# The last layer's self-attention with its two heads on the two halves of the array's rows, the maxima added by a bf16 matmul, and the key sums on GpSimd

## What is computed

```python
def _L1_attn_ref(x, w_q, w_k, w_v, w_o):          # 16 heads, d_k = 64, no mask
    scale = 1.0 / sqrt(64)
    q = einsum('bsd,hdk->bhsk', x, w_q)           # k and v alike
    scores = einsum('bhqk,bhmk->bhqm', q, k) * scale
    weights = softmax(scores, axis=-1)
    z = einsum('bhqm,bhmk->bhqk', weights, v)
    z = transpose(z, (0, 2, 1, 3)).reshape(b, s, h * dk)
    return x + einsum('bse,ed->bsd', z, w_o)
```

## Time and profile before

| | us |
|---|---|
| timed runs, median of 3 (lowest, highest) | 914.5 (913.91, 914.62) |
| the profiled execution | 905.64 |
| its span in the trace | 903.8 |
| of it, the loop of stage d and its output (from L1218's first to L1316's start) | 366.5 to 650.8 |
| busy in the span: PE, DVE, ACT, POOL | 804.2, 563.1, 302.9, 126.6 |
| mean granted clock of TensorE in the profiled execution | 0.932 of full speed |

### The profile page before, as it was taken

The page is one execution under the profiler, slowest core; times in us unless marked ns, Lnnn a source line. Parts: engine busy times, 40 slices in busy tenths (PEclk is TensorE's granted clock), DMA queues, the critical chain, the costliest instruction groups (busy, mean ns, idle before and its releaser), DMA issues.

```text
span 903.8 us, 8453 instructions
## 1 busy us (share of the span) xinstructions
PE 804.2 (89%) x3018; PEld 390.6 (43%) x3018; DVE 563.1 (62%) x1288; ACT 302.9 (34%) x499; POOL 126.6 (14%) x116
## 2 busy tenths in 40 slices
PE   7528788879999999999999999999898698999996
PEld 4214563466665433322322322232464235466665
DVE  5979799544155494457878778778654654433334
ACT  3360656600321105434544554553103221312220
POOL 0796221300010011000000000000035310000000
PEclk9858599999997899869999999999999798999999
DMA  8000000000500000000000000000031000000000
GB/s 344 25 1 0 1 1 2 1 1 0 213 1 1 0 1 0 1 0 0 1 0 1 1 0 1 0 1 0 1 126 73 1 1 1 0 1 1 0 1 24
DMA packets 3491, 18.64 MB, mean 21 GB/s; under 512 B 887, under 2 KB 2040, under 8 KB 2938
## 3 DMA queue, kind: packets, MB, share of 16 engines
q1 hardware_dynamic: 3450, 18.11, 5.0%
HBM read 17.58 MB, written 0.52 MB: 20 GB/s over the span
## 4 chain that ended last, share of the span: by engine, by line
PE 63%; DVE 22%; POOL 6%; ACT 5%; issue 3%; DMA 0%; POOLq 0%; DVEq 0%; SPq 0%; ACTq 0%
PE PS L1759 9%; PE PS L1218 8%; DVE SB L1429 6%; PE PS L1231 5%; PE PS L1773 5%; PE PS L1185 4%; PE PS L1198 3%; PE PS L215 2%; DVE SB L1388 2%; DVE SB L1134 2%; PE PS L639 2%; PE PS L1316 2%; PE PS L1247 2%; PE PS L662 2%; PE PS L1557 1%
## 5 line engine op out<-in xcount | busy, mean ns | idle before, releaser
L1218 PE MATMUL PS<-SB 68*128 68x512 f32 x256 | 128.6, 627 | 0.0
L195 POOL TENSOR_TENSOR SB<-SB 128x4 f32<-128x4 f32 (+1 forms) x26 | 25.9, 996 | 676.9 <-DVE SB L179 676.7
L215 PE MATMUL PS<-SB 128*128 128x512 f32 (+1 forms) x232 | 108.8, 617 | 5.0 <-ACT SB L511 3.5
L1378 DVE TENSOR_REDUCE SB<-PS 128x2 f32<-128x1024 f32 x64 | 78.3, 1224 | 54.0 <-PE PS L1198 54.0
L1343 ACT ACTIVATE SB<-PS 128x1024 f32<-128x1024 f32 x64 | 65.5, 1023 | 92.1 <-PE PS L1218 90.7
L1759 PE MATMUL PS<-SB 128*128 128x512 f32 x176 | 82.5, 607 | 0.0
L1231 PE MATMUL PS<-SB 128*64 128x512 f32 x256 | 70.4, 629 | 7.7 <-DVE SB L1433 7.7
L1218 PEld LDWEIGHTS PS<-SB 68*128 68x128 f32 x256 | 46.3, 195 | 60.5 <-issue 59.2
L215 PEld LDWEIGHTS PS<-SB 128*128 128x128 f32 x232 | 45.3, 214 | 50.3 <-issue 43.0
L1839 DVE TENSOR_TENSOR SB<-SB,PS 128x512 f32<-128x512 f32 (+1 forms) x48 | 32.8, 688 | 52.7 <-PE PS L1759 49.1
L1429 DVE RECIPROCAL SB<-PS 128x512 f32<-128x512 f32 x16 | 53.7, 3358 | 7.5 <-PE PS L1247 7.0
(11 more groups left out here) (350 smaller groups left out, 1124.9 us busy)
## 6 DMA issues: line engine op xcount, KB each, us to landing
SB<-exp SPq DMA_DIRECT2D x1, 4352.0 KB, 13.3
SB<-moe SPq DMA_DIRECT2D x1, 4096.0 KB, 13.0
SB<-dft SPq DMA_DIRECT2D x1, 2304.0 KB, 11.4
SB<-att SPq DMA_DIRECT2D x1, 2048.0 KB, 16.7
SB<-mix SPq DMA_DIRECT2D x1, 768.5 KB, 4.2
SB<-mix SPq DMA_DIRECT2D x1, 640.0 KB, 5.3
SB<-ssm SPq DMA_DIRECT2D x1, 602.0 KB, 6.4
SB<-lat SPq DMA_DIRECT2D x1, 585.0 KB
```

The costliest lines, as they stand in the source:

```text
L215: pe.matmul(bank(b)[:, 0:moving.shape[1]], ones, moving, start=True, stop=True)
L1218: ins = pe.matmul(bank(2 * (n % 2) + k), two_heads(k_ring[i % 3])[0:DK + 4, h, 128 * kt:128 * kt + 128], two_heads(q_ring[i % 3])[0:DK + 4 ...
L1378: dve.tensor_reduce(shift[i % 2][:, qt:qt + 5:4], two_heads(bank(4, 2)), AX_X, ALU.max, negate=True)\
```

## The change

The two heads of a pair now stay on the partitions on which the projection leaves them, 0 to 63 and 64 to 127. ACT copies bank 7 twice, to bf16 and to f32, with no move between partitions. A score step u takes key tile u of both heads: two f32 matmuls on the two halves of the array's rows, and then two bf16 matmuls (64 rows of ones times shift_rows) into the same banks, which add the maxima. The maxima's transpose is one of 128 x 128 (shift has the columns of the first head from 0, of the second from 64, the rest zero), and DVE multiplies it with own_tile into shift_rows, all 128 partitions at once. expd is ordered by key tile, so the key sum of a pair is three additions of 1024 columns, which are now on GpSimd. PE's order changes: maxima 0, 2, 3 come right behind the scores, ahead of project and weigh, and weigh 0 comes behind maxima 1. DVE keeps its order without the key sums.

```diff
@@ -1149,10 +1149,11 @@
     D2 = Space(W2.end, END)
     headed = D2(8192)
     expd = [D2(4096) for _ in range(2)]
-    q_ring, k_ring = [D2(1024) for _ in range(3)], [D2(1024) for _ in range(3)]
-    qb_ring, kb_ring = [D2(512, BF16) for _ in range(3)], [D2(512, BF16) for _ in range(3)]
-    half_sum, key_sum, unit = D2(1024), D2(1024), D2(512)
-    shift = [D2(8) for _ in range(2)]
+    q_ring, k_ring = [D2(512) for _ in range(3)], [D2(512) for _ in range(3)]
+    qb_ring, kb_ring = [D2(256, BF16) for _ in range(3)], [D2(256, BF16) for _ in range(3)]
+    half_sums, key_sum, unit = [D2(1024) for _ in range(2)], D2(1024), D2(512)
+    shift, shift_rows = [D2(128) for _ in range(2)], [D2(256, BF16) for _ in range(2)]
+    own_tile, ones_16 = D2(4), D2(64, BF16)
     NP_ = B * PAIRS
 
     ctx_n, ctx_T, ctx_kv = lat["ctx"], xn[:, 0:512], att["w_v"]
@@ -1189,34 +1190,33 @@
             n = 4 * i + qt
             if qt == 0:
 
-                pe.wait_ge(sem("d_bf16"), 2 * i + 2)
+                pe.wait_ge(sem("d_qk_in"), 4 * i + 4)
                 if i >= 1:
                     pe.wait_ge(sem("d_shift_in"), i)
             if n >= 1:
                 pe.wait_ge(sem("d_max"), n)
             for h in range(2):
-                ins = pe.matmul(bank(4 + h), two_heads(qb_ring[i % 3])[0:DK, h, 128 * qt:128 * qt + 128],
-                                two_heads(kb_ring[i % 3])[0:DK, h, :], start=True, stop=True)
+                ins = pe.matmul(bank(4 + h), qb_ring[i % 3][head(h), 128 * qt:128 * qt + 128], kb_ring[i % 3][head(h), :],
+                                start=True, stop=True)
             ins.then_inc(sem("d_rough"), 1)
 
         def shifts(i):
 
             pe.wait_ge(sem("d_max"), 4 * i + 4)
-            for h in range(2):
-                ins = pe.transpose(bank(4)[0:4, 128 * h:128 * h + 128], shift[i % 2][:, 4 * h:4 * h + 4], ident)
-            ins.then_inc(sem("d_shifts"), 1)
+            pe.transpose(bank(4)[:, 0:128], shift[i % 2], ident).then_inc(sem("d_shifts"), 1)
 
         def score(i, u):
-            h, half = divmod(u, 2)
             n = 4 * i + u
             if u == 0:
                 pe.wait_ge(sem("d_shift_in"), i + 1)
             if n >= 2:
                 pe.wait_ge(sem("d_exp"), n - 1)
-            for k in range(2):
-                kt = 2 * half + k
-                ins = pe.matmul(bank(2 * (n % 2) + k), two_heads(k_ring[i % 3])[0:DK + 4, h, 128 * kt:128 * kt + 128],
-                                two_heads(q_ring[i % 3])[0:DK + 4, h, :], start=True, stop=True)
+            for h in range(2):
+                pe.matmul(bank(2 * (n % 2) + h), k_ring[i % 3][head(h), 128 * u:128 * u + 128], q_ring[i % 3][head(h), :],
+                          start=True, stop=False)
+            for h in range(2):
+                ins = pe.matmul(bank(2 * (n % 2) + h), ones_16[head(h), :], shift_rows[i % 2][head(h), :],
+                                start=False, stop=True)
             ins.then_inc(sem("d_scores"), 1)
 
         def weigh(i, kt):
@@ -1228,7 +1228,7 @@
                     pe.wait_ge(sem("d_headed"), i)
             for h in range(2):
                 v = value[:, 1024 * (4 * b + kt) + 128 * pair + DK * h:1024 * (4 * b + kt) + 128 * pair + DK * h + DK]
-                ins = pe.matmul(bank(6)[DK * h:DK * h + DK, :], v, expd[i % 2][:, 2048 * h + 512 * kt:2048 * h + 512 * kt + 512],
+                ins = pe.matmul(bank(6)[head(h), :], v, expd[i % 2][:, 1024 * kt + 512 * h:1024 * kt + 512 * h + 512],
                                 start=(kt == 0), stop=(kt == 3))
             if kt == 3:
                 ins.then_inc(sem("d_weighed"), 1)
@@ -1273,11 +1273,11 @@
                 project(1, 1)
             if 2 <= t < 6:
                 maxima(0, t - 2)
+        pe.wait_ge(sem("d_ones"), 3)
         shifts(0)
         stay_warm(pe, 3, 5)
         pe.wait_ge(sem("d_v_even"), NT // 2)
         pe.wait_ge(sem("d_v_odd"), NT // 2)
-        pe.wait_ge(sem("d_ones"), 3)
         for i in range(NP_ + 1):
             now, ahead, before = i < NP_, i + 1 < NP_, i >= 1
 
@@ -1286,14 +1286,12 @@
                     shifts(i + 1)
                 if now:
                     score(i, u)
-                if ahead and u in (0, 2):
-                    maxima(i + 1, (0, None, 3)[u])
-                if before:
-                    weigh(i - 1, u)
-                if ahead and u == 1:
-                    maxima(i + 1, 2)
+                if ahead and u < 3:
+                    maxima(i + 1, (0, 2, 3)[u])
                 if i + 2 < NP_ and u < 2:
                     project(i + 2, u)
+                if before and u:
+                    weigh(i - 1, u)
                 if i == NP_ - 2 and u == 1:
                     pe.wait_ge(sem("e_ctx_n"), 1)
                     pe.wait_ge(sem("d_unit"), NP_ - 3)
@@ -1304,6 +1302,8 @@
                     context(u)
                 if ahead and u == 0:
                     maxima(i + 1, 1)
+                if before and u == 0:
+                    weigh(i - 1, 0)
                 if before and u == 2:
                     sums(i - 1)
         for t in range(NT):
@@ -1329,11 +1329,8 @@
 
                 act.wait_ge(sem("d_scores"), 4 * (i - 2))
             act.wait_ge(sem("d_qk"), 2 * i + which + 1)
-            for h in range(2):
-                act.activation(two_heads(ring[i % 3])[0:DK, h, :], bank(7)[DK * h:DK * h + DK, :], ACT.Copy, scale=s)\
-                   .then_inc(sem("d_qk_in"), 1)
-            act.wait_ge(sem("d_qk_in"), 4 * i + 2 * which + 2)
-            act.activation(low[i % 3][0:DK, :], ring[i % 3][0:DK, :], ACT.Copy).then_inc(sem("d_bf16"), 1)
+            act.activation(low[i % 3], bank(7), ACT.Copy, scale=s).then_inc(sem("d_qk_in"), 1)
+            act.activation(ring[i % 3], bank(7), ACT.Copy, scale=s).then_inc(sem("d_qk_in"), 1)
 
         def exp(i, u):
             if i >= 2 and u == 0:
@@ -1362,8 +1359,20 @@
     def d_pool(pool):
 
         pool.wait_ge(sem("stage_done"), 3)
-        for r in k_ring:
-            pool.memset(r[DK:DK + 4, :], 1.0).then_inc(sem("d_ones"), 1)
+        pool.memset(ones_16, 1.0).then_inc(sem("d_ones"), 1)
+        for s in shift:
+            pool.memset(s, 0.0).then_inc(sem("d_ones"), 1)
+
+        for i in range(NP_):
+            for half in range(2):
+                pool.wait_ge(sem("d_exp"), 4 * i + 2 * half + 2)
+                e = expd[i % 2][:, 2048 * half:2048 * half + 2048]
+                pool.tensor_tensor(half_sums[half], e[:, 0:1024], e[:, 1024:], ALU.add).then_inc(sem("d_half_sum"), 1)
+            pool.wait_ge(sem("d_half_sum"), 2 * i + 2)
+            if i >= 1:
+                pool.wait_ge(sem("d_sums"), i)
+            pool.tensor_tensor(key_sum, half_sums[0], half_sums[1], ALU.add).then_inc(sem("d_key_sum"), 1)
+            pool.wait_ge(sem("d_key_sum"), i + 1)
 
     def d_dve(dve, follow):
         def v_in(t):
@@ -1375,31 +1384,20 @@
             dve.wait_ge(sem("d_rough"), n + 1)
             if qt == 0 and i >= 2:
                 dve.wait_ge(sem("d_shifts"), i - 1)
-            dve.tensor_reduce(shift[i % 2][:, qt:qt + 5:4], two_heads(bank(4, 2)), AX_X, ALU.max, negate=True)\
+            dve.tensor_reduce(shift[i % 2][:, qt:qt + DK + 1:DK], two_heads(bank(4, 2)), AX_X, ALU.max, negate=True)\
                .then_inc(sem("d_max"), 1)
 
         def shift_in(i):
 
             dve.wait_ge(sem("d_shifts"), i + 1)
-            if i >= 3:
-                dve.wait_ge(sem("d_scores"), 4 * (i - 2))
-            per_tile = lambda a: a.rearrange("p (h c) -> p h c", h=2)[:, :, None, :].to_broadcast([4, 2, 4, 128])
-            own = ident[0:4, None, 0:4, None].to_broadcast([4, 2, 4, 128])
-            dve.tensor_tensor(q_ring[i % 3][DK:DK + 4, :].rearrange("p (h t c) -> p h t c", h=2, t=4),
-                              per_tile(bank(4)[0:4, 0:256]), own, ALU.mult).then_inc(sem("d_shift_in"), 1)
-
-        def key_sums(i, h):
-            dve.wait_ge(sem("d_exp"), 4 * i + 2 * h + 2)
-            if h == 0 and i >= 1:
-                dve.wait_ge(sem("d_sums"), i)
-            e = expd[i % 2][:, 2048 * h:2048 * h + 2048]
-            follow(dve.tensor_tensor(half_sum, e[:, 0:1024], e[:, 1024:], ALU.add))
-            ins = dve.tensor_tensor(two_heads(key_sum)[:, h, :], half_sum[:, 0:512], half_sum[:, 512:], ALU.add)
-            if h:
-                ins.then_inc(sem("d_key_sum"), 1)
-            else:
-                follow(ins)
-
+            if i >= 2:
+                dve.wait_ge(sem("d_scores"), 4 * (i - 1))
+            dve.tensor_tensor(shift_rows[i % 2].rearrange("p (t c) -> p t c", t=4),
+                              bank(4)[:, None, 0:128].to_broadcast([P, 4, 128]),
+                              own_tile[:, :, None].to_broadcast([P, 4, 128]), ALU.mult).then_inc(sem("d_shift_in"), 1)
+
+        follow(dve.tensor_tensor(own_tile, ident[:, 0:4], ident[:, DK:DK + 4], ALU.add))
+        dve.wait_ge(sem("d_ones"), 3)
         v_in(1)
         maximum(0, 0)
```

(7 more changed lines are left out.)

## The result

The changed kernel takes 860.84 us in the median of four runs (853.79 to 866.99), the kernel before 914.45: a ratio of 0.939 (95% interval 0.930 to 0.948). The ratio leaves out the run of 866.99, which counts as a slow one because it lies over 1.5% above the fastest. In six more runs on another occasion the median was 866.31 against 913.65, ratio 0.946 (0.943 to 0.950). The executions of the changed kernel fall in two groups, near 855 and near 866, and the first figure is a middle between them. Of the two groups there is one profile each, and what parts these two lies ahead of the stage that the change touches: stage d begins (its first L207) at 351.30 us in the execution of 866.73 and at 338.49 in the one of 853.79.

A forecast was written before the change was run, and what follows sets the result against it. The prediction took the circle through the reciprocal, 14.9 us a pass, as the bound; gains of 1.0, 2.3, 3.9, 27.6 and 4.2 summed to 39.0 us, taken from the median 914.5 for 876, range 865 to 890.

The forecast's parts named there:

- the term of the clock: TensorE's clock in the stage: one fall, as now, at another place, priced at 8.1 us, so the sum stands.
- the carrying over to the median: From the profiled 905.64 us to the timed median 914.5, 8.9 above: the same 39 us taken off, giving 875.5.
- The bound and the circle: Loop pass: circle from maxima 1 through shifts, reciprocal, product and maximum, 14.9 us; PE waits before project (0.4) and maxima 1 (0.9).
- Scores and maxima side by side: PE slots on two row halves: a score slot with its bf16 pair 1.27 us, a maxima slot 0.31 against 0.53.
- rival F: GpSimd's key-sum adds in the loop take over 4.9 us, against 2.35 expected, and set the pass; chance 0.01.
- Ahead of the loop and the first passes: Before the twelve passes: gains of about 1.0 us ahead of the loop, 2.3 in the first pass, 3.9 in the second.
- D: Loop: kernel slower, the clock falling again and again, each fall taking back 8.1 us; chance 0.05.
- E: Loop: row halves don't run side by side when groups around them differ; 17.9 us a pass, 924 in all; chance 0.01.
- G: Loop: the circle through the reciprocal is shorter and PE's 13.6 us sets the pass, giving 859; chance 0.03.
- The last passes: Loop end without projection: last intervals 11.8 and 8.3 us against 13.86 and 9.18; 4.2 us gained with the pass ahead.
- Rival C: Stage: one or two clock falls more than now, from the two long waits at the loop's end, 884 to 892; chance 0.24.
- rival B: Stage: no clock fall at all, since the rows are full, giving 868; chance 0.18.

The follow-up runs named there:

- the run on one half: Changed kernel with both heads' maxima taken from the first head's rows, 864.99 us; for E, both heads' score and shift matmuls on the first 64 rows instead, 918.61 us.
- the doubled adds: Changed kernel with each of GpSimd's three key-sum adds issued a second time into a tile nobody reads: 877.46 us, passes of 14.55.
- before's second profile: The kernel before, unchanged, profiled again: 912.71 us, with the stretch near 242 us and a fall of 10.2 us in the loop's first pass.
- the run with full rows: Kernel before with its score matmuls over all 128 rows instead of 68: 909.23 us against 913.65, ratio 0.9943; passes of 17.20.
- the second score ahead: Changed kernel with the second score right behind maxima 0, ahead of project, maxima 1 and weigh 0: median 851.45 us against 866.31; passes of 13.38.

## Why the prediction was right and wrong

Forecast were 876 us and a gain of 39 in the stage; measured were 860.84. Of the 15.2 us between them 8.3 lie in the stage, which gave 47.3 us in the comparison above: 4.9 by the clock, and 3.4 by the rest of it (4.2 more than forecast in the twelve passes, 0.5 more ahead of them, 1.3 less in the last ones). Another 5.5 are the mixture of the two groups in the first four runs (860.84 against 866.31), and the rest is the spread of the medians and rounding. The steps that failed are the term of the clock, which was put at no change, and the carrying over to the median; the slots of the circle were a little too long.

**The bound and the circle: right.** A pass is not PE's work but the circle through the reciprocal; the two waits stand where they were named, released by what was named, and moving one score out of the circle takes them away. The length was 14.55, not 14.9. By terms: PE's part from maxima 1 to the shifts is 8.24 us instead of 8.42, because a score that a maxima pair follows takes 1.18 (465.47 to 466.65), not the 1.27 of the cross attention's, which weigh follows. DVE's part is 6.31 instead of 6.47: 0.37 for 0.41 to L1395, and 0.61 for 0.72 from there to the reciprocal, since the reciprocal starts before the 0.69 us of L1395 are over. The 12 passes gave 31.8 us, not 27.6: 4.2 us of the miss.

**Scores and maxima side by side: right**, 1.28 us with weigh behind it, 0.31 for maxima (0.53 without, by the run on one half).

**GpSimd hides: right.** An add takes 2.35 us, and rival F's point of 4.9 us an add is about where the doubled adds (4.7) stood, and the passes held.

**Ahead of the loop and the first passes: right.** 7.2 us were forecast without the clock. Measured are 12.6, and 7.7 without the 4.9 of the fall. The parts were less good than their sum: up to the first score 1.3 for 1.0 (26.56 us from L207 in before's second profile, 25.27 after), the first pass 2.6 for 2.3, the second 3.1 for 3.9. The second pass before is 15.5 us at full clock (L1390 of the run with full rows, 388.32 to 403.83), not 16.8.

**The other rivals.** D, the clock falling again and again in the loop, did not come: no fall in the twelve passes of any profile. E is what the run on one half shows, by taking the halves apart. G gave PE's work 13.6 us, and it is 13.4; it becomes the pass only once the second score is moved.

**The last passes: 2.9 instead of 4.2.** The wait ahead of the last weigh is 2.07 us (2.1 forecast), and behind it the clock falls, 3.4 us at 591.8: the last interval is 9.70 instead of 8.3. Rival C's mechanism, in the small. The other long wait, in the pass without projects (2.20 us at 566.00, 2.4 forecast), left the clock up.

**The clock: the first step that failed.** I had the right row, half-filled rows ahead of the fall, and gave it a chance of 0.18 (rival B); the forecast counted on one fall in the stage, "as now, at another place", and so put the clock at nothing in the sum. Taken by its words there is one fall, at another place, but it is one of 3.4 us in place of 10.2 or 20.5, and the sum had given all falls one price. The two pairs of profiles that differ in the rows alone show that the fall of the first pass needs the half-filled rows at these moments: 4.9 us in executions like the second profile, 9.8 in those like the first. I also priced it at 8.1 by laying the second pass, with a fall, against a later one of 17.20; at full clock that pass is 15.5, and the fall costs 9.8. And I read the row at 645.21 wrongly: the clock held over that wait of 1.43 us, but among the work ahead of it was a score on 68 rows:

```profile
640.79 1.98 PE L1218 MATMUL PS<-SB 68*128 68x512 f32 x4
```

**The median: the second step that failed.** I carried the profiled sum over to the median by adding 8.9 us, and did not ask what they are. All timed runs of the kernel before but one (907.10) lie between 912.3 and 914.9, so the profile of 905.64 was of a rare execution. The second profile of before accounts for 7.1 of them: 9.7 more ahead of the stage (L207 at 349.65 and 339.95; 9.3 of it by the stretch near 242 us, 3.4 ahead of it, 3.0 less behind it), 4.8 less from the shorter fall in the first pass, and 2.2 more behind the stage. Of the first four runs of the changed kernel two lie in the group near 855 (one of them is the profiled one, without the stretch), so the median came out 5 us below that of the group near 866. Forecast were 39 from the stage; measured are 42.4 by the same stretches (7.7, 31.8, 2.9), and 4.9 of the clock besides. Against the group with the stretch, 866.3, the point was 10 us too high, half from the clock and most of the rest from the passes; that this would still lie in the range, by 1.3 us, would have been luck, for the clock was priced at nothing.

## What to carry to other kernels

When an engine's work shrinks, write down the circle that remains (from a wait back to itself, across engines) with its slots; parts of the change that lie off it, here GpSimd's key sums, can then be seen to be worth nothing before anything is built. A new order of the work can be priced in the same way (here it cost 0.08 us a pass), and the next gain is whatever can be taken out of the circle and put into its waits. Heads on row halves pay by running side by side, 1.06 us for each score step here, and all of the gain of a pass hung on that. Before a sum from one profile is added to a median, look for what parts the two: here falls of the clock in stages ahead, which together are as large as a fifth of the gain.

## What the runs showed of the hardware

TensorE's clock fell behind a wait of 1.32 us when the matmuls ahead of it used 68 and 64 rows, and held behind the same wait, 0.2 us later in the program, when the scores used all 128, 60 of them filled with zeros and ones; a second pair of profiles shows the same. So the rows that a matmul covers seem to matter for the clock, not only the time that PE is busy. It is not shown which of the values and the covered rows does it, nor that the rows decide by themselves: with half-filled rows and the same wait 1.6 us later the clock held, and with full rows it fell once behind a wait of 1.32 us in the first pass (the second score ahead, 385.2). Behind one and the same wait of 2.20 us it held in the changed kernel and fell with the doubled adds. In the loop a fall lasted 3.4, 10.2 or 20.5 us with PE busy throughout. It cost half of that: 1.6, 4.9 and 9.8 us.

In the changed kernel's passes PE waits 0.36 and 0.74 us each time, and in none of the twelve did the clock fall, in any of the profiles. The Trainium skill ("TensorE: Matmul & The Clock Gate", section "A second HAM failure mode: psum-queue depth-cycling") warns that short idles repeated between groups of matmuls can make the clock go to and fro. The twelve passes here, with two such waits each, do not show it, and the fall in the first pass of the kernel before is a single one, not a going to and fro. The page measured another kernel; for this one the measurement decides.
